# A quantised feed-forward kernel: one comparison moved from VectorE to GpSimd, three small scales made later, and nine filler matmuls in the first steps

## The reference

```python
c = einsum('bsd,bdh->bsh', x, W[itok]) + b[itok][:, None, :]
w_scale = mean(abs(weight)) + EPS                       # ffn weight, 512 x 512
w_quant = clip(round(weight / w_scale), -1.0, 1.0)
a_scale = max(abs(c), axis=-1, keepdims=True) + EPS
a_quant = round(clip(c / a_scale * 127.0, -128.0, 127.0))
y = einsum('bsi,oi->bso', a_quant, w_quant) * (w_scale * a_scale / 127.0)
out = x + y
```

## Time and profile before

| | us |
|---|---|
| median of 3 runs | 500.98 |
| lowest and highest | 500.81, 501.63 |
| the profiled execution | 500.77 |
| its span | 498.8 |
| TensorE busy | 488.7 (98%) |
| GpSimd busy | 383.6 (77%) |
| VectorE busy | 354.7 (71%) |
| ScalarE busy | 334.8 (67%) |

### The profile page before, as it was taken

One profiled execution on the slowest core, in us unless ns is written; L12 is line 12 of the kernel. 1 busy time (PEld: TensorE's weight loads), 2 busy tenths in 40 slices (PEclk: granted clock), 3 DMA queues, 4 the chain that ended last, 5 costly groups with the idle time before them and its releaser, 6 DMA issues.

```text
span 498.8 us, 13132 instructions
## 1 busy us (share of the span) xinstructions
PE 488.7 (98%) x2183; PEld 360.9 (72%) x2217; DVE 354.7 (71%) x654; ACT 334.8 (67%) x502; POOL 383.6 (77%) x399
## 2 busy tenths in 40 slices
PE   8889999999999999999999999999999999999997
PEld 3667777777777777777777777777777777777774
DVE  6657686487865797887766869855978587566854
ACT  3657666687767676768656687765877667467642
POOL 7768797588976798897776879866988688676850
PEclk9989999999999999999999999999999999999999
DMA  7789997999989999999989999999999999799943
GB/s 249 264 265 384 362 353 283 342 400 384 365 318 379 365 412 399 415 407 411 370 297 339 327 394 411 407 337 337 415 408 408 341 396 332 232 380 330 333 154 144
DMA packets 71730, 172.69 MB, mean 346 GB/s; under 512 B 8097, under 2 KB 8354, under 8 KB 71586
## 3 DMA queue, kind: packets, MB, share of 16 engines
q1 hardware_dynamic: 53714, 139.88, 76.2%
q10 hardware_dynamic: 18000, 32.64, 17.8%
HBM read 138.94 MB, written 33.55 MB: 346 GB/s over the span
## 4 chain that ended last, share of the span: by engine, by line
PE 93%; issue 0%; DVE 0%; DVEq 0%
PE ps_cond L749 23%; PE ps_cond L747 23%; PE ps_cond L748 23%; PE ps_y L700 22%; PE ps_aT L711 3%; PE ps_cond L700 0%; DVE sb_x_rows L609 0%; DVE sb_x_rows L654 0%; DVEq L43 0%
## 5 line engine op out<-in xcount | busy, mean ns | idle before, releaser
L363 POOL TENSOR_TENSOR sb_xT_lo<-sb_xT_raw,sb_xT_hi 128x512 fp32r<-128x512 f32 x128 | 166.2, 1299 | 97.8 <-PE ps_cond L749 92.4
L747 PE MATMUL ps_cond<-sb_w_hi,sb_xT_hi 128*128 (+1 forms) x512 | 225.9, 441 | 0.1
L749 PE MATMUL ps_cond<-sb_w_hi,sb_xT_lo 128*128 (+1 forms) x512 | 201.6, 394 | 0.0
L748 PE MATMUL ps_cond<-sb_w_lo,sb_xT_hi 128*128 (+1 forms) x512 | 199.9, 390 | 0.0
L623 DVE TENSOR_REDUCE sb_absmax<-ps_cond 128x1 f32<-128x512 f32 x128 | 87.6, 684 | 88.9 <-PE ps_cond L749 86.9
L388 POOL TENSOR_SCALAR sb_y_scale<-sb_absmax,sb_w_step 128x1 f32<-128x1 f32 x128 | 143.0, 1118 | 7.3 <-DVE sb_absmax L623 6.5
L408 ACT ACTIVATE ps_cond<-sb_w_raw 128x512 f32 x127 | 75.7, 596 | 91.4 <-issue 59.4
L577 DVE TENSOR_TENSOR sb_w_lo<-sb_w_raw,sb_w_hi x106 | 126.4, 1230 | 9.1 <-issue 8.5
L700 PE MATMUL ps_y<-sb_ffnT,sb_aT 128*128 128x512 bf16 x471 | 122.5, 380 | 2.9 <-DVEq L583 1.2
L747 PEld LDWEIGHTS ps_cond<-sb_w_hi,sb_xT_hi 128*128 128x128 f32 x512 | 96.7, 189 | 30.9 <-issue 0.7
L492 ACT ACTIVATE sb_a_rounded<-ps_cond,sb_a_inv 128x512 int8<-128x512 f32 x128 | 87.7, 685 | 46.3 <-DVE sb_a_inv L629 45.6
(11 more groups left out here) (88 smaller groups left out, 49.6 us busy)
## 6 DMA issues: line engine op xcount, KB each, us to landing
sb_w_raw<-cond_wb SPq DMA_DIRECT2D x53, 768.0 KB, 7.7
sb_xT_raw<-x_t SPq DMA_DIRECT2D x128, 256.0 KB, 5.8
sb_x_rows<-x SPq DMA_DIRECT2D x128, 256.0 KB, 5.8
out<-sb_x_rows ACTq DMA_DIRECT2D x124, 256.0 KB, 5.6
sb_w_raw<-cond_wb SPq DMA_DIRECT2D x53, 512.0 KB, 5.9
sb_w_raw<-cond_wb SPq DMA_DIRECT2D x5, 256.0 KB, 3.9
sb_ffn_raw<-ffn_t SPq DMA_DIRECT2D x1, 1024.0 KB, 7.2
out<-sb_x_rows SPq DMA_DIRECT2D x3, 256.0 KB, 2.1
```

The source lines that it names most:

```text
L363: pool.tensor_tensor(xT_lo[:, m, :], xT_raw[:, m, :], xT_hi[:, m, :].bitcast(F32), ALU.subtract).then_inc(x_lo_done, 1)
L747: pe.matmul(ps_cond, x_hi_k, w_hi_k, start=(start and k == 0), stop=False, skip_group_check=True)
L748: pe.matmul(ps_cond, x_hi_k, w_lo_k, start=False, stop=False, skip_group_check=True)
L749: last_mm = pe.matmul(ps_cond, x_lo_k, w_hi_k, start=False, stop=(k == KD - 1), skip_group_check=True)
```

## The change

Three edits. GpSimd, and no longer VectorE, compares the raw ffn weight with `half_down`; it does so at the end of its step 0, behind the `xT_hi` of step 3, and is released by a new semaphore `halves_there`. GpSimd makes no scale in steps 0, 1 and 2; in step 3 it makes those of steps 0, 1 and 2 and then its own (`SCALES_FROM = 3`), for which `absmax` and `y_scale` get eight columns instead of four. TensorE runs three matmuls of zeros into bank `y_ps[1]` ahead of the first transpose, three ahead of the second transpose and three ahead of the first second product (`BUSY_FIRST = 3`).

```diff
-    X_AHEAD, SEED_AHEAD, T_BEHIND, Y_BEHIND, STORE_BEHIND = 2, 3, 2, 3, 4
+    X_AHEAD, SEED_AHEAD, T_BEHIND, Y_BEHIND, STORE_BEHIND, SCALES_FROM = 2, 3, 2, 3, 4, 3
...
-    BUSY, BUSY_BEHIND = 20, 4
+    BUSY, BUSY_BEHIND, BUSY_FIRST = 20, 4, 3
...
-        absmax = sb("absmax", [P, STAT_RING])
+        absmax = sb("absmax", [P, U])
...
-        y_scale = sb("y_scale", [P, STAT_RING])
+        y_scale = sb("y_scale", [P, U])
...
+            def scale_of(step, n):
+                pool.wait_ge(absmax_done, step + 1)
+                pool.sem_inc(absmax_taken, 1)
+                pool.tensor_scalar(y_scale[:, n:n + 1], absmax[:, n:n + 1], EPS, w_step[:, 0:1],
+                                   ALU.add, ALU.mult).then_inc(y_scale_done, 1)
+
             def body(r0, u, first, last):
                 r = r0 + u
 
                 pool.wait_ge(cond_mm_done, r + 1)
                 if not last or u + X_AHEAD < U:
                     split_x_low(r + X_AHEAD, (u + X_AHEAD) % U)
-                s = u % STAT_RING
+                if first and u == SCALES_FROM:
+                    pool.wait_ge(ffn_scaled, 1)
+                    for step in range(SCALES_FROM):
+                        scale_of(step, step)
+                if not first or u >= SCALES_FROM:
+                    scale_of(r, u)
+                if not last or u + X_AHEAD + 1 < U:
+
+                    split_x_high(r + X_AHEAD + 1, (u + X_AHEAD + 1) % U)
                 if first and u == 0:
-                    pool.wait_ge(ffn_scaled, 1)
-                pool.wait_ge(absmax_done, r + 1)
-                pool.sem_inc(absmax_taken, 1)
-                pool.tensor_scalar(y_scale[:, s:s + 1], absmax[:, s:s + 1], EPS, w_step[:, 0:1],
-                                   ALU.add, ALU.mult).then_inc(y_scale_done, 1)
-                if not last or u + X_AHEAD + 1 < U:
-
-                    split_x_high(r + X_AHEAD + 1, (u + X_AHEAD + 1) % U)
+                    pool.wait_ge(halves_there, 1)
+                    pool.tensor_scalar(ffn_minus[:, :], ffn_raw[:, :], half_down[:, 0:1], None,
+                                       ALU.is_lt).then_inc(ffn_minus_done, 1)
...
                 done()
-                dve.tensor_scalar(ffn_minus[:, :], ffn_raw[:, :], half_down[:, 0:1], None,
-                                  ALU.is_lt).then_inc(ffn_minus_done, 1)
+                dve.sem_inc(halves_there, 1)
...
+            def busy(bank, count):
+                for _ in range(count):
+                    pe.matmul(bank[:, :], zeros[:, 0:P], zeros[:, :], start=True, stop=True)
+
...
             def behind(r, u, first):
                 if not first or u >= T_BEHIND:
+                    if first and u < T_BEHIND + 2:
+                        busy(y_ps[1], BUSY_FIRST)
                     a_transpose(r - T_BEHIND, (u - T_BEHIND) % U, first)
                 if not first or u >= Y_BEHIND:
+                    if first and u == Y_BEHIND:
+                        busy(y_ps[1], BUSY_FIRST)
                     second_product(r - Y_BEHIND, (u - Y_BEHIND) % U, first)
```

More of the change, by code:

```diff
@@ L150, in adaln_ffn @@
         ffn_minus_done = sem("ffn_minus_done")
+        halves_there = sem("halves_there")
         ffn_ternary = sem("ffn_ternary")
@@ L382, in body @@
                     split_x_low(r + X_AHEAD, (u + X_AHEAD) % U)
-                s = u % STAT_RING
-                if first and u == 0:
+                if first and u == SCALES_FROM:
                     pool.wait_ge(ffn_scaled, 1)
-                pool.wait_ge(absmax_done, r + 1)
-                pool.sem_inc(absmax_taken, 1)
-                pool.tensor_scalar(y_scale[:, s:s + 1], absmax[:, s:s + 1], EPS, w_step[:, 0:1],
-                                   ALU.add, ALU.mult).then_inc(y_scale_done, 1)
+                    for step in range(SCALES_FROM):
+                        scale_of(step, step)
+                if not first or u >= SCALES_FROM:
+                    scale_of(r, u)
                 if not last or u + X_AHEAD + 1 < U:
                     split_x_high(r + X_AHEAD + 1, (u + X_AHEAD + 1) % U)
+                if first and u == 0:
+                    pool.wait_ge(halves_there, 1)
+                    pool.tensor_scalar(ffn_minus[:, :], ffn_raw[:, :], half_down[:, 0:1], None,
+                                       ALU.is_lt).then_inc(ffn_minus_done, 1)
             over_steps(pool, body)
@@ L604, in result @@
             def result(step, n):
-                s = n % STAT_RING
                 dve.wait_ge(y_mm_done, step + 1)
@@ L608, in result @@
                 dve.wait_ge(rows_loaded[n], rows_landed(step, n))
-                dve.scalar_tensor_tensor(x_rows[:, n, :], y_bank(step, n)[:, :], y_scale[:, s:s + 1],
+                dve.scalar_tensor_tensor(x_rows[:, n, :], y_bank(step, n)[:, :], y_scale[:, n:n + 1],
                                          x_rows[:, n, :], ALU.mult, ALU.add).then_inc(y_done, 1)
@@ L622, in body @@
                     dve.wait_ge(bias0_added, 1)
-                dve.tensor_reduce(absmax[:, s:s + 1], cond_ps[u % COND_BANKS][:, :], AX.X, ALU.max,
+                dve.tensor_reduce(absmax[:, u:u + 1], cond_ps[u % COND_BANKS][:, :], AX.X, ALU.max,
                                   apply_absolute_value=True).then_inc(absmax_done, 1)
                 dve.wait_ge(absmax_done, r + 1)
-                dve.tensor_scalar(a_step[:, s:s + 1], absmax[:, s:s + 1], EPS, 1.0 / LEVELS,
+                dve.tensor_scalar(a_step[:, s:s + 1], absmax[:, u:u + 1], EPS, 1.0 / LEVELS,
                                   ALU.add, ALU.mult).then_inc(a_step_done, 1)
@@ L650, in _ @@
             dve.wait_ge(rows_loaded[U - 1], rows_landed(B - 1, U - 1))
-            s = (B - 1) % STAT_RING
+            s = U - 1
             for half in range(2):
```

## The result

The changed kernel takes 503.59 us (median of 8 runs, 502.74 to 505.44); the kernel before takes 500.36 in the runs beside them (8 runs, 498.47 to 501.63). The ratio is 1.0069, 95% interval 1.005 to 1.0087: slower, where I had forecast a gain of 1.5 us and a range that ended at 502.3.

A forecast was written before the change was run, and what follows sets the result against it. TensorE's matmuls bound the body of the run; only the first 32 us could change. 500.77 - 1.5 (clock held) + 0.1 (step 4) = 499.4, 499.6 at the median's level, stated as 499.5; 8-in-10 range 499.0 to 502.3.

The forecast's parts named there:

- the duration of the comparison: GpSimd's comparison of 2048 columns, starting at 17.75, takes about 2.1 us, like a one-input cast.
- my upper bound of 5.1: Comparison on GpSimd at the two-input subtraction's rate: about 4.6 us, or 5.1 by plain ratio.
- the slow case: Rival: slow GpSimd comparison; at 3.5 us the kernel takes 500.5, at 4.8 the clock falls, 502.3; chance 0.17.
- Behind the comparison: GpSimd's remainder of step 3 runs 19.8 to 21.1, in time for TensorE's step 3 at 21.42.
- the later case of the first rival: VectorE's L577 slips in too; remainder of step 3 ends at 24.6, time 502.6; whole rival's chance 0.27.
- the case of 501.9: VectorE takes the port first at 19.85; remainder of step 3 ends at 23.2, a loss of 0.9; rival's chance 0.27.
- the signs of being wrong: In the profile after: comparison over 2.6 us, remainder of step 3 over 2, step 3 past 22, or clock 0.5.
- Who is first at the port: At the comparison's end, 19.85, GpSimd's remainder of step 3 narrowly starts before VectorE's L601, by about 0.09 us.
- if a gap goes: TensorE's filler groups cost nothing inside gaps of 1.0 to 1.17; without its gap one costs 0.65, all three 1.95.
- The fall at 27 us: TensorE sinks to 1.2 GHz behind the gaps, losing 1.2 us in step 4 and a little in the second product.
- The timeline of a cured kernel: With TensorE's clock held at 2.4 GHz, the transpose of step 2 comes at 30.5 instead of 32.04, 1.5 us gained.

The follow-up runs named there:

- The dose: Comparison columns on GpSimd varied over 0, 512, 1024 and 2048 in the changed kernel, the rest on VectorE: ratios 0.9987, 0.9988, 1.0029, 1.0069.
- The quarter: Changed kernel with 512 of the 2048 columns compared on GpSimd, the rest on VectorE: 499.43 us, ratio 0.9988 to the kernel before.
- the comparison on VectorE: Changed kernel with the comparison moved back to VectorE, fillers and late scales kept: 499.75 us, ratio 0.9987 to the kernel before.

## Why the prediction was wrong

**The step that failed** is the duration of the comparison: "It has one tensor operand, so I take 2.1, end 19.85." It took 5.44 and ended at 23.26, above even my upper bound of 5.1. The bound from above was the nearer one, the subtraction's 1.27 for 512 columns. I chose the cast's row because both operations read one tensor, with nothing to show that GpSimd's time goes by that; no row had this instruction in more than one column. The two estimates from the Trainium skill, "GPSIMD Engine Reference", section 3.1, 2.0 and 3.3 us, are both too low; the measurement decides. That choice gave the slow case 0.17 of the chance and priced its end at 502.3, with a comparison 0.6 us too short and fillers that cost nothing. It also took that case's path through the remainder of step 4, at 28.8 and 1.3 later. With the slower comparison that remainder ended at 29.34, and it was not what bounded: TensorE, with step 3 at 1.2 GHz, started step 4 only at 32.14.

**Behind the comparison**, the chain up to step 3 was as described. The remainder of step 3 is next and TensorE's step 3 waits for it; it decides from a remainder's end past some 21.4, not from 21.4 + 1.2 as the prediction had it. The dose shows it: no loss at 21.22, 1.0 us of waiting at 22.7, 3.2 at 24.5. The stall's size and effect are those of the later case of the first rival, whose remainder ends at 24.6, though its cause is another. That case was priced too low by the prediction's own sum: the remainder ends 1.4 later than in the case of 501.9, which makes 503.3 and not 502.6, and 503.59 was measured. Of the signs of being wrong three came (the comparison over 2.6 us, step 3 past 22, a clock of 0.5) and one did not (the remainder of step 3 took 1.26).

**Who is first at the port** came out as forecast, by as little: GpSimd's remainder starts at 23.25, 0.01 ahead of the comparison's end, and takes its normal 1.26; VectorE's L610 starts at 23.30 and takes 3.36 instead of 2.33, ending 2.15 after the remainder. VectorE did not get in first in any profile with a comparison that it waited for.

**The fillers** were sized right (0.22 each), and their cost "if a gap goes" was in the text, but the slow case was not charged with it. Six of them did fall on the path. Leaving them out took 1.4 us off that stretch in one profile, but not off the median (1.0085); their net cost is open.

**The clock** is where the mechanism was right and the sum too simple. The fall at 27 us costs about what I took from the rows; I charged the kernel before with it in every execution. It occurs in 21 of 60 runs. A cure is worth some 2.2 x 0.35 = 0.8 us on average, not 1.5, near what the three kernels with fillers and no stall show by their medians (0.7, 0.85 and 1.0 us under before). So even with a comparison of 2.1 us the forecast gain would have been about twice too large. The quarter is close to that case: its comparison on GpSimd took 2.26 us and hid, and the gain was 0.85. The timeline of a cured kernel was right: with the late scales alone and the clock held, the transpose of step 2 comes at 30.51, and 30.5 was forecast.

**What I left out:** that taking the comparison off VectorE frees nothing. By the timeline its reduction of step 1 began at 19.74 before and begins at 20.01 now, behind 2.30 us of sequencer work (two table reads of some 0.75 each and a branch, with waits) under which the comparison had been hidden.

No version was clearly faster than the kernel before. The fillers alone (0.9983), the comparison on VectorE (0.9987) and the quarter (0.9988) lie together below it, each with an interval that reaches just past 1; what they do show clearly is no run with a fallen clock (0 of 36, against 21 of 60).

## What to carry to other kernels

Before work is moved to another engine, ask for a row of that very instruction form at that size on that engine; where there is none, take the dearest row, and let the queue behind it decide whether that is still harmless. Look at what hides the work where it stands: on an engine whose sequencer is busy anyway it may be free. And a clock that falls in one profiled execution is a chance, not a constant: count it over all runs before charging it.

## What the runs showed of the hardware

- GpSimd's tensor_scalar of 128x2048 takes 5.4 us for a comparison and a multiplication alike, with either kind of scalar and to bf16 or fp32; its cast and its copy of the same size take 1.89, and VectorE takes 1.29 for the comparison.
- TensorE's clock falls behind idle gaps of about 1 us in one profile and not behind equal ones in another. 21 of 60 runs of the kernel before have a lower mean, and a median 2.2 us higher than the rest. In the kernels with nine filler matmuls in these gaps it is 0 of 36.
- Through an idle stretch of 3.17 us the clock sank to 1.2 GHz in one execution of the changed kernel, and through one of 2.82 it stayed at 2.4 GHz in another. The twelve matmuls behind it took 5.29 and 2.86 us.
- A pair of two-input operations on VectorE takes 2.37 us where the two run back to back, and 3.8 where one of GpSimd's gets in between the halves. Which of the two it is changes over a run: with the fillers alone three pairs between 110 and 140 us take 3.8, most of the others 2.37.
